# Macaron block (MoE feed-forward, recurrent attention, MoE feed-forward): queries laid out over a dimension of 16, one query load a step, copies, weights and merges issued elsewhere, a new order of the work

## The chip, the core and the metric

One core of a Trainium2 chip runs the whole kernel as one program. The engines are TensorE (PE in the profile, its weight loads PEld), VectorE (DVE), ScalarE (ACT), GpSimd (POOL) and SyncE (SP). SP, ACT and POOL can issue DMAs; the bytes are moved by 16 DMA engines of the core. The metric is the time of one execution on the device in microseconds, the median of several runs.

## The reference, cut to what matters

x is (4, 512, 512) float32. The block is x + 0.5 FFN(LN(x)), then + attention(LN(x)), then + 0.5 FFN(LN(x)).

```python
# FFN: top-2 of E=8 experts with gates, and a shared expert beside them
logits = xf @ gate_w; top2, softmax over the two
h = gelu(xf @ w1[e] + b1[e]);  routed = sum over the two of gate * (h @ w2[e] + b2[e])
shared = gelu(xf @ shared_w1 + shared_b1) @ shared_w2 + shared_b2
# attention: K=32 heads, HH=8 values each, M=8 frequencies, KQ=4 query groups of 8 heads
z = causal_conv4(x @ W_mem);  k_val = z[..., :256], s_raw = z[..., 256:]
q = (x @ W_q).reshape(b, l, 4, 8, 8, 2)                 # group, h, m, re/im
p_w = exp(clip(scale * s_raw, -20, 20) + log_w)          # one weight per head and position
re, im = cumsum(p_w * cos(k_val * theta)), cumsum(p_w * sin(k_val * theta))   # for each m
out_re = sum_m(re * q_re + im * q_im) / den;  out_im = sum_m(im * q_re - re * q_im) / den
y = out_re @ W_re + out_im @ W_im;  (y_val * silu(y_gate)) @ W_out
```

A query group is repeated for its 8 heads: every row of q is used by 8 rows of (head, h).

## The kernel before, in words

**Jobs and groups.** A feed-forward of one batch (512 rows, four tiles of 128) is a job; jobs 0 to 3 are the first feed-forward of batches 0 to 3, jobs 4 to 7 the second. A job fetches its rows into `xin`, normalises them, stores them to DRAM (`x_normal`), turns them, computes the gates and the shared expert (`hidden`, `acc`), and stores the shared part to `sum_rows`. Jobs form groups ([0], [1], [2], [3], [4, 5], [6, 7]) whose rows are sorted by expert into 15 or 23 blocks of 128 rows. For each block POOL gathers rows (`bring`, into three buffers `xs`), TensorE turns them (`x`), multiplies (`one`, L887), turns (`mid`), multiplies (`two`, L903), ACT copies between these, and POOL adds the scaled result to rows in DRAM (`add`, L1698), alternately to `x_rows` and `sum_rows`. The planes `x_rows` begin as copies of x (`w_rows`, L1952), 1 MB for a batch.

**Attention of a batch.** SP loads the rows (`a_load`), POOL adds `sum_rows` to them (`a_add`) and also in DRAM (`m_rows`, L1710, 1 MB read and accumulated). After the norm TensorE makes the memory input (`a_mem`, L922) and the queries (`a_q`, L931), whose weights share one tile `turns_sb` with the output weights, so these are loaded again in turn (`w_head`, L1894 and L1895, and `w_tail`, L1900, on SP). The queries of a group leave TensorE as 128 rows (m, h, re/im); ACT keeps them in `xin`, and SP stores them to DRAM (`q_cols`, L1867) in four DMAs of 256 KB a batch. `xin` is used in turn by jobs and attention (the list `TURNS`), so the next fetch into it waits for these stores.

**Steps.** Then 16 steps (two halves of heads, 8 frequencies) for each batch, 64 in all, one stream on VectorE: phases, ACT's sine and cosine, two scans (L1474), the products with the queries (L1481, L1486), the sums (L1497 to L1507). For each step SP loads `qx` (128 partitions: 2 groups x 8 heads x 8 h; 4 KB each) from `q_cols` in two DMAs of 64 partitions (L1882), each reading 8 different rows 8 times over. After 8 steps the half is scaled by the denominators (`c_out`), moved (L1888) and goes through the gate (`o_gate`, L956) and, after both halves, the output rows (`o_rows`, L965), which POOL adds to `x_rows`. The last job sums them in place.

**Order.** All work is declared as pieces with an engine, a cost, and what they wait for (`plan_job`, `plan_blocks`, `plan_head`, `plan_step`, `plan_tail`); `orders()` lists them for each engine by the length of the way behind them, plus numbers from the table `URGENT`. Each engine executes its list in order; the real waits are on semaphores. Lines that the change and the argument touch most:

```python
# store of a query group, destination in DRAM (SP, L1867)
bass.AP(q_dram, (b % 2 * KQ + q) * P * T, [[T, 2], [2 * T, M * HH], [1, T]])
# load for a step, for g in range(QH) (SP, L1881, L1882)
bass.AP(q_dram, q * P * T + m * HH * 2 * T, [[0, KPQ], [2 * T, HH], [1, 2 * T]])
# normal rows to DRAM (SP, L1845): the same tile xin, [[D, P], [1, D]] as destination
# merge of a batch (POOL): waits for a_loaded[0..3] alone
```

Of the kernel before, what the change touches and what calls it, by code (L numbers as in the profile page):

```python
# [61 lines left out]
def macaron(nc, x, small, gate_w, sw1, sw2, b2_rows, w_experts, w_mem, w_q, w_bd, w_out, out):  # L62
# [43 lines left out]
    with ctx:  # L106
# [146 lines left out]
        q_dram = nc.dram_tensor("q_cols", (2, KQ, M, HH, 2, T), F32)  # L253
# [7 lines left out]
        def batch_rows(dram, b):  # L261
            if isinstance(dram, list):
# [13 lines left out]
                 ("a_load", 2), ("fetch", 4), ("fetch", 5), ("a_load", 3), ("fetch", 6), ("fetch", 7)]  # L276
        work = {}
# [20 lines left out]
        def plan_weights():  # L298
# [8 lines left out]
            piece("SP", ("w_bd",), 0.5, ("PE", ("one", 0, 2)))  # L307
# [3 lines left out]
            for b in range(B):  # L311
                piece("SP", ("w_rows", b), 0.5, ("PE", ("one", 0, 2)) if b >= len(GROUPS[0]) else ("SP", ("w_expert", E - 1)))

        def plan_job(q):
# [10 lines left out]
            piece("POOL", ("load", q), 3.6, ("DVE", ("load", q)))  # L325
# [82 lines left out]
        def plan_head(b):  # L408
            rows, turned_rows = rows_free(("a_load", b))
            if b != 1:  # L410
                piece("SP", ("w_head", b), 0.9, *([("PE", ("o_rows", b - 2, TB - 1))] if b else [("SP", ("w_bd",))]))
            weights = ("SP", ("w_head", 0 if b == 1 else b), 12.0)
# [3 lines left out]
            piece("POOL", ("m_rows", b), 1.0, ("POOL", ("a_add", b, TB - 1)))  # L416
            piece("DVE", ("a_stats", b), 3.4, *[("POOL", ("a_add", b, tb), 4.6 - 0.8 * (TB - 1 - tb)) for tb in range(TB)])
            piece("POOL", ("a_stats", b), 3.6, ("DVE", ("a_stats", b)))
# [31 lines left out]
        def plan_step(i):  # L450
# [3 lines left out]
            piece("SP", ("c_query", b, n), 1.2, *[("SP", ("a_q", b, half * QH + g), 2.5) for g in range(QH)], *free)  # L454
# [8 lines left out]
        def plan_tail(b):  # L463
            if b + 1 < B:
                piece("SP", ("w_tail", b), 0.5, ("PE", ("a_q", b + 1, KQ - 1)), ("PE", ("a_mem", b + 1, 1)))
# [19 lines left out]
            for tb in range(TB):  # L485
                s = ("o_rows", b, tb)
                piece("PE", s, 5.3, ("DVE", ("o_mul", b, VT - 1)), ("SP", ("w_tail", min(b, B - 2)), 15.0),
# [7 lines left out]

        URGENT = {
            ("ACT", "a_q"): {3: 23},
            ("ACT", "a_turn"): {1: 4},
            ("ACT", "acc"): {3: 198},
            ("ACT", "mid"): {1: -298, 3: 19},  # L500
            ("ACT", "o_gate"): {3: -413},
            ("ACT", "one"): {2: 333, 4: -1832},
            ("ACT", "two"): {1: -181, 2: -85},
            ("ACT", "x"): {2: 15, 4: 303},
            ("DVE", "a_stats"): {2: -822},
            ("DVE", "c_sum"): {0: -149, 1: 110, 2: 558, 3: 528},
            ("DVE", "c_times"): {0: -682, 3: 191},
            ("DVE", "c_turn"): {1: -1124, 2: -139},
            ("DVE", "rows"): {2: 217},
            ("PE", "a_mem"): {0: 35, 1: -6, 2: -1076},  # L510
            ("PE", "a_turn"): {1: -815, 2: -510},
            ("PE", "c_out"): {0: -821},
            ("PE", "chunks"): {4: -79, 5: -367},
            ("PE", "gT"): {6: 198},
            ("PE", "hidden"): {2: -6},
            ("PE", "logits"): {6: -852},
            ("PE", "mid"): {0: 271, 1: 960, 3: -444, 4: 344},
            ("PE", "o_rows"): {0: -882, 3: 225},
            ("PE", "one"): {2: 10, 4: -323, 5: -359},
            ("PE", "place"): {1: -674},  # L520
            ("PE", "turn"): {1: 602, 4: 22},
            ("PE", "two"): {1: -8, 3: -104},
            ("PE", "x"): {0: 3, 2: 966, 3: 10, 4: -517, 5: 247},
            ("POOL", "add"): {1: -372},
            ("POOL", "bring"): {1: -163},
        }

# [482 lines left out]
        def scalar_program():  # L1010
# [160 lines left out]

            for stage, *at in ORDERS["ACT"]:
                if stage == "turn":
                    keep_x(*at)
                elif stage == "chunks":
                    keep_chunks(*at)
                elif stage == "gates":
# [879 lines left out]
```

## Time and profile before

| | |
|---|---|
| median of 3 runs | 1193.39 us (1191.97 to 1195.2) |
| the profiled execution, its own time | 1190.12 us |
| its span, first to last instruction | 1188.9 us |
| mean granted TensorE clock | 0.943 |
| TensorE busy | 1024.6 us (86%) |
| VectorE busy | 729.8 us (61%) |
| ScalarE busy | 631.0 us (53%) |
| GpSimd busy | 487.2 us (41%) |

The shares are means over stages that differ: VectorE has no attention steps before 212 us and none behind 954 us, where the last job and the last group are left. Times in the views are us from the start of the span. The granted clock is 1.00 at 2.4 GHz and 0.5 at 1.2 GHz; a mean between them says how much of a stretch was at each level.

### The profile page before, as it was taken

How to read it: one execution, taken by the hardware profiler on the slowest of the kernel's cores; microseconds unless marked ns; L12 is line 12 of the kernel's file. 1: busy time of each engine (PE TensorE's matmuls, PEld its weight loads, DVE VectorE, ACT ScalarE, POOL GpSimd, SP SyncE). 2: the span in 40 equal slices, each digit the busy share in tenths (PEclk: the TensorE clock that was granted, in tenths of full speed). 3: DMA queues.
4: the chain of work that ended last, by engine and by line, in shares of the span. 5: the costliest groups of instructions: out<-in, count | busy, mean ns of one | idle time of the engine just before them, and what ended most of it. 6: DMA issues, size and time to landing. Idle time of an engine off the chain costs nothing.

```text
span 1188.9 us, 11370 instructions
## 1 busy us (share of the span) xinstructions
PE 1024.6 (86%) x3424; PEld 569.3 (48%) x3424; DVE 729.8 (61%) x1210; ACT 631.0 (53%) x1090; POOL 487.2 (41%) x451
## 2 busy tenths in 40 slices
PE   5987989888879979979499989898987899989993
PEld 2465635555344444435255534445453554436661
DVE  2310116878889989879679888998998931200000
ACT  4343325648556588355366574436778852224451
POOL 3434451454553334532432231534363523155642
PEclk9988999998999989989799899898998999999997
DMA  9876571657864666873565757246687645426757
GB/s 311 325 245 158 78 168 49 154 135 159 169 170 105 166 164 109 182 197 107 141 154 117 187 118 178 60 123 180 108 199 164 145 67 77 110 66 130 122 94 113
DMA packets 68977, 172.54 MB, mean 145 GB/s; under 512 B 12354, under 2 KB 12354, under 8 KB 66790
## 3 DMA queue, kind: packets, MB, share of 16 engines
q0 software_dynamic: 32576, 72.44, 33.9%
q1 hardware_dynamic: 36342, 99.38, 27.6%
q8 instruction: 30, 0.49, 0.2%
q14 instruction: 29, 0.24, 0.1%
HBM read 112.86 MB, written 68.33 MB: 152 GB/s over the span
## 4 chain that ended last, share of the span: by engine, by line
PE 29%; DMA 23%; DVE 16%; issue 12%; POOL 11%; ACT 7%; SPq 1%; POOLq 0%; DVEq 0%; ACTq 0%
PE hps L887 8%; PE yps L903 7%; DMA xs<-x_normal,rows_i 4%; DMA x_rows<-ys,rows_i 3%; DMA q_cols<-xin 3%; PE misc L965 3%; DMA xin<-in_x 3%; DVE run L1474 2%; PE xps L878 2%; PE yps L845 2%; DMA qx<-q_cols 2%; PE misc L931 2%; POOL slots L1660 2%; DVE trig L1481 2%; DMA xin<-sum_rows 2%
## 5 line engine op out<-in xcount | busy, mean ns | idle before, releaser
L887 PE MATMUL hps<-w_all,hidden_sb 128*128 x848 | 215.0, 399 | 16.5 <-ACT hidden_sb L1069 13.6
L1674 POOL DMA_INDIRECT xs<-x_normal,rows_i x106 | 128.3, 1210 | 227.8 <-PE xps L878 169.2
L903 PE MATMUL yps<-w_all,hidden_sb 128*128 x424 | 207.8, 614 | 5.7 <-ACT hidden_sb L1069 5.7
L887 PEld LDWEIGHTS hps<-w_all,hidden_sb 128*128 128x128 f32 x848 | 164.5, 201 | 58.1 <-issue 38.4
L1474 DVE TENSOR_TENSOR_SCAN run<-pwx,trig 128x512 f32<-128x512 f32 x128 | 149.5, 1210 | 23.8 <-ACT trig L1157 15.9
L1698 POOL DMA_INDIRECT x_rows<-ys,rows_i x56 | 96.0, 1714 | 118.7 <-ACT ys L1082 112.4
L833 PE MATMUL hps<-xnT,sw_sb 128*128 128x512 f32 x256 | 117.9, 610 | 9.2 <-ACT hidden_sb L1042 9.2
L845 PE MATMUL yps<-sw_sb,hidden_sb 128*128 128x512 f32 x256 | 121.6, 619 | 0.0
L1082 ACT ACTIVATE ys<-yps,slots 128x512 f32<-128x512 f32 x106 | 73.0, 689 | 89.8 <-PE yps L903 72.5
L878 PE MATMUL xps<-ident,xs 128*128 128x128 f32 x424 | 69.7, 292 | 54.5 <-DMA xs<-x_normal,rows_i 25.9
L903 PEld LDWEIGHTS yps<-w_all,hidden_sb 128*128 128x128 f32 x424 | 80.7, 198 | 74.5 <-issue 71.0
L878 PEld LDWEIGHTS xps<-ident,xs 128*128 128x128 f32 x424 | 54.4, 150 | 90.8 <-issue 54.9
L1660 POOL DMA_INDIRECT slots<-told,dest_i x64 | 66.8, 1044 | 57.1 <-DVE cmp_a L1343 38.8
L965 PE MATMUL misc<-turns_sb,tail_sb 128*128 128x512 f32 x192 | 85.3, 593 | 1.8 <-DVE tail_sb L1535 1.7
L1698 POOL DMA_INDIRECT sum_rows<-ys,into_i x28 | 49.6, 1771 | 90.4 <-ACT ys L1082 85.2
L1481 DVE TENSOR_TENSOR trig<-run,qx 128x1024 f32<-128x1024 f32 x64 | 78.0, 1219 | 8.3 <-DMA qx<-q_cols 8.0
L833 PEld LDWEIGHTS hps<-xnT,sw_sb 128*128 128x128 f32 x256 | 48.6, 195 | 70.7 <-issue 59.0
L1060 ACT COPY hidden_sb<-hps 128x256 f32<-128x256 f32 x106 | 39.0, 371 | 78.2 <-PE hps L887 78.0
L1486 DVE TENSOR_TENSOR qx<-run,qx 128x1024 f32<-128x1024 f32 x64 | 78.0, 1218 | 0.0
L845 PEld LDWEIGHTS yps<-sw_sb,hidden_sb 128*128 128x128 f32 x256 | 47.3, 195 | 56.8 <-issue 56.8
L1069 ACT ACTIVATE hidden_sb<-hps,bias_of 128x128 f32<-128x128 f32 x212 | 65.7, 367 | 15.7 <-PE hps L895 15.2
L1052 ACT COPY hidden_sb<-xps 128x512 f32<-128x512 f32 x106 | 62.0, 588 | 19.7 <-PE xps L878 10.9
(202 smaller groups left out, 1530.4 us busy)
## 6 DMA issues: line engine op xcount, KB each, us to landing
qx<-q_cols SPq DMA_DIRECT2D x128, 256.0 KB
w_all<-in_w_experts SPq DMA_DIRECT2D x8, 1024.0 KB, 10.2
x_normal<-xin SPq DMA_DIRECT2D x32, 256.0 KB, 4.2
xin<-x_rows SPq DMA_DIRECT2D x32, 256.0 KB, 7.1
turns_sb<-in_w_out SPq DMA_DIRECT2D x3, 1536.0 KB, 11.5
xin<-in_x SPq DMA_DIRECT2D x16, 256.0 KB, 6.2
sum_rows<-ys SPq DMA_DIRECT2D x16, 256.0 KB, 5.7
xin<-sum_rows POOLq DMA_DIRECT2D x16, 256.0 KB, 8.4
```

The costliest lines, as they stand in the source:

```text
L833: t = PE.matmul(hps[:, bank, :], sw1_sb[:, c, n * P:(n + 1) * P], xnT[:, c, :], start=c == 0, stop=c == KC - 1)
L845: t = PE.matmul(yps[:, bank, :], hT[:, n, tb * P:(tb + 1) * P], sw2_sb[:, n, :], start=False, stop=n == SC - 1)
L878: t = PE.transpose(xps[:, bank, c * P:(c + 1) * P], xs[:, j % NX, c * P:(c + 1) * P], ident[:, :])
L887: t = PE.matmul(hps[:, bank, 0:H], xT[:, j % 2, c, :], w_all[:, bass.ds(expert[j] + c * H, H)], start=c == 0, stop=c == KC - 1)
L903: t = PE.matmul(yps[:, bank, :], hb[:, j % 2, ec, :], w_all[:, bass.ds(expert[j] + (KC * H + ec * D), D)], start=ec == 0, stop=ec == EC - 1)
L965: t = PE.matmul(misc[:, bank, :], yT[:, v, tb * P:(tb + 1) * P], wout_sb[:, v, :], start=v == 0, stop=v == VT - 1)
L1474: t = VE.tensor_tensor_scan(run[:, c, :], pwx[:, n // M, :], trig[:, n % 2, c, :], 0.0, ALU.mult, ALU.add)
L1481: VE.tensor_tensor(trig[:, n % 2, :, :], run[:, :, :], qx[:, n % NQX, :, :], ALU.mult).then_inc(*real_made.of((b, n)))
L1486: VE.tensor_tensor(qx[:, n % NQX, :, :], back, qx[:, n % NQX, :, :], ALU.mult).then_inc(*imag_made.of((b, n)))
L1660: GE.indirect_dma_start(slots_dram[g], bass.IndirectOffsetOnAxis(dest_i[:, g % 2, t, r:r + 1], 0), told[:, g % 2, first_tile + t, r, :], N ...
L1674: GE.indirect_dma_start(xs[:, j % NX, :], None, xn_rows[PAIR_OF[g]], bass.IndirectOffsetOnAxis(rows_i[:, g % 2, j:j + 1], 0)).then_inc(*xs ...
L1698: GE.indirect_dma_start(INTO[g][side], bass.IndirectOffsetOnAxis(at[:, g % 2, j:j + 1], 0), ys[:, j % 2, :], None, compute_op=ALU.add).the ...
```

## The change

1. `q_cols` is laid out as (half, m, group in half, h, re/im, T), so that a store's destination begins with 16 rows (h, re/im) and then 8 (m), and a step's source is 16 rows, each repeated for 8 partitions: one load of 128 partitions and 512 KB instead of two. Partitions of the attention are now ordered (group, h, head) instead of (head, h); the columns of W_mem, taps, theta, norm, W_re and W_im are permuted on the host and the replication matrix `rep_sb` is built with one pass per copy instead of two.
2. The copies of x to `x_rows` for batches 1 to 3 were issued together behind block 2 of group 0; they now stand behind block 8 of group 0, and blocks 2 and 8 of group 1 (the copy to x_normal stays with batch 3's). `bring` waits for that copy only in groups of the second pair of batches. `w_bd` is loaded behind the first attention turn.
3. `w_head` and `w_tail` are issued by ACT instead of SP.
4. `m_rows` on POOL waits for the batch's step 2 besides.
5. `URGENT` is replaced by new numbers, with two further tables (`KINDS` for a kind of piece, `PARTS` for a part of the kernel and its batch), and some costs are changed; so every engine's order is drawn anew.

```diff
-        q_dram = nc.dram_tensor("q_cols", (2, KQ, M, HH, 2, T), F32)
+        q_dram = nc.dram_tensor("q_cols", (2, HALVES, M, QH, HH, 2, T), F32)
+        ROWS_BEHIND = {1: (0, 8), 2: (1, 2), 3: (1, 8)}
...
-            piece("SP", ("w_bd",), 0.5, ("PE", ("one", 0, 2)))
+            piece("SP", ("w_bd",), 0.5, ("PE", ("a_turn", 0, TB - 1)))
...
-                piece("SP", ("w_rows", b), 0.5, ("PE", ("one", 0, 2)) if b >= len(GROUPS[0]) else ("SP", ("w_expert", E - 1)))
+                piece("SP", ("w_rows", b), 0.5, ("PE", ("one", *ROWS_BEHIND[b])) if b in ROWS_BEHIND else ("SP", ("w_expert", E - 1)))
...
-            piece("POOL", ("load", q), 3.6, ("DVE", ("load", q)))
+            piece("POOL", ("load", q), 3.6 if q < 2 else 5.2, ("DVE", ("load", q)))
...
-                piece("SP", ("w_head", b), 0.9, *([("PE", ("o_rows", b - 2, TB - 1))] if b else [("SP", ("w_bd",))]))
-            weights = ("SP", ("w_head", 0 if b == 1 else b), 12.0)
+                piece("ACT", ("w_head", b), 0.4, ("PE", ("o_rows", b - 2, TB - 1) if b else ("one", 0, 2)))
+            weights = ("ACT", ("w_head", 0 if b == 1 else b), 14.0)
...
-            piece("POOL", ("m_rows", b), 1.0, ("POOL", ("a_add", b, TB - 1)))
+            piece("POOL", ("m_rows", b), 1.5, ("POOL", ("a_add", b, TB - 1)), ("DVE", ("c_scan", b, 3)))
...
-            piece("SP", ("c_query", b, n), 1.2, *[("SP", ("a_q", b, half * QH + g), 2.5) for g in range(QH)], *free)
+            piece("SP", ("c_query", b, n), 0.7, *[("SP", ("a_q", b, half * QH + g), 2.5) for g in range(QH)], *free)
...
+        def urgency(k):
+
+            engine, stage, at = k[0], k[1][0], k[1][1] if len(k[1]) > 1 else 0
+            return (URGENT.get((engine, stage), {}).get(at, 0.0) + KINDS.get((engine, stage), 0.0)
+                    + PARTS.get(PART_OF.get(stage), {}).get(at, 0.0))
...
+            def load_head_weights(b):
+                if b > 0:
+                    act.wait_ge(*rows_made.at((b - 2, TB - 1)))
+                else:
+                    act.wait_ge(*one_made.at((0, 2)))
+                SE.dma_start(wmem_sb, w_mem).then_inc(*head_loaded.of((b, 0)))
+                SE.dma_start(wq_sb, w_q).then_inc(*head_loaded.of((b, 1)))
...
-                if g > 0:
+                if PAIR_OF[g]:
                     pool.wait_ge(*rows_filled.at(B - 1))
...
             def merge_rows(b):
+                pool.wait_ge(*scanned.at((b, 2)))
...
-                SP.dma_start(bass.AP(q_dram, (b % 2 * KQ + q) * P * T, [[T, 2], [2 * T, M * HH], [1, T]]),
-                             xin[:, q, :]).then_inc(*q_stored[q].of(b))
+                half, g = divmod(q, QH)
+                into = bass.AP(q_dram, ((b % 2 * HALVES + half) * M * QH + g) * HH * 2 * T,
+                               [[T, 2 * HH], [QH * HH * 2 * T, M], [1, T]])
+                SP.dma_start(into, xin[:, q, :]).then_inc(*q_stored[q].of(b))
...
-                for g in range(QH):
-                    q = b % 2 * KQ + half * QH + g
-                    src = bass.AP(q_dram, q * P * T + m * HH * 2 * T, [[0, KPQ], [2 * T, HH], [1, 2 * T]])
-                    SP.dma_start(qx[g * KPQ * HH:(g + 1) * KPQ * HH, s, :, :], src).then_inc(*q_loaded[s].of((b, n, g)))
+                src = bass.AP(q_dram, ((b % 2 * HALVES + half) * M + m) * QH * HH * 2 * T,
+                              [[2 * T, QH * HH], [0, KPQ], [1, 2 * T]])
+                SP.dma_start(qx[:, s, :, :], src).then_inc(*q_loaded[s].of((b, n)))
...
-                    sp.wait_ge(*one_made.at((0, 2)))
+                    sp.wait_ge(*a_turned.at((0, TB - 1)))
...
-                    if at[0] >= len(GROUPS[0]):
-                        sp.wait_ge(*one_made.at((0, 2)))
+                    if at[0] in ROWS_BEHIND:
+                        sp.wait_ge(*one_made.at(ROWS_BEHIND[at[0]]))
```

## Rows read from the trace of the kernel before

**Rows 1.** Busy times by stretch: PE, PEld, DVE, ACT, POOL, clock, DMA share, GB/s.

```profile
0.00:954.00 954.00, 818.84 (x2689) 449.65 (x2690) 708.62 (x1124) 544.46 (x913) 393.43 (x367) 0.94 0.64 157
218.00:954.00 736.00, 631.06 (x2042) 341.91 (x2041) 652.19 (x955) 458.17 (x753) 305.20 (x242) 0.94 0.63 147
954.00:1188.90 234.90, 205.75 (x738) 119.65 (x736) 21.15 (x87) 86.58 (x178) 93.76 (x84) 0.97 0.53 97
```

**Rows 2.** The chain that ended last, shares of the span by engine.

```profile
PE 29%; DMA 23%; DVE 16%; issue 12%; POOL 11%; ACT 7%; SPq 1%; POOLq 0%; DVEq 0%; ACTq 0%
```

**Rows 3.** The chain in order of time: start us, us, what; nine transfers.

```profile
71.92 10.68 DMA x_rows<-ys,rows_i
83.64 13.99 DMA x_rows<-ys,rows_i
...
160.52 11.15 DMA xs<-x_normal,rows_i
...
201.62 9.30 DMA q_cols<-xin
...
240.00 9.39 DMA q_cols<-xin
249.40 10.12 DMA xin<-in_x
...
340.95 8.87 DMA qx<-q_cols
...
395.60 12.43 DMA xin<-in_x
...
556.07 20.19 DMA q_cols<-xin
```

**Rows 4.** DMA issues: count, KB each, median us from issue to landing.

```profile
x_normal<-xin SPq DMA_DIRECT2D x32, 256.0 KB, 4.2
...
xin<-in_x SPq DMA_DIRECT2D x16, 256.0 KB, 6.2
...
x_rows<-sum_rows POOLq DMA_DIRECT2D x4, 1024.0 KB, 14.6
...
xs<-x_normal,rows_i POOLq DMA_INDIRECT x106, 5.3
...
x_rows<-ys,rows_i POOLq DMA_INDIRECT x56, 5.3
```

**Rows 5.** Waits of VectorE: us in total, times, longest us.

```profile
DVE stats_ffn L1237 <- DMA xin<-in_x: 9.5, 5, 6.4
DVE trig L1481 <- DMA qx<-q_cols: 8.0, 3, 3.5
```

**Rows 6.** SP's issues in order of time, 540 to 560 us.

```profile
543.64 5.21 SPq L1867 DMA_DIRECT2D q_cols<-xin  x2
...
554.23 5.15 SPq L1867 DMA_DIRECT2D q_cols<-xin  x2
```

**Rows 7.** VectorE in order of time, with idle time before and its releaser.

```profile
576.93 2.76 DVE L1237 BATCH_NORM_STATS2 stats_ffn<-xin 128x6 f32<-128x512 f32 x4 [10.60 <-DMA xin<-x_rows]
...
611.88 1.23 DVE L1474 TENSOR_TENSOR_SCAN run<-pwx,trig 128x512 f32<-128x512 f32 x1 [7.21 <-ACT pwx L1148]
```

**Rows 8.** TensorE in order of time, at its longest stall.

```profile
594.26 1.08 PE L878 MATMUL xps<-ident,xs 128*128 128x128 f32 x4 [17.62 <-issue]
```

**Rows 9.** Instructions on qx and on x_rows: ns min/median/max, first and last start.

```profile
L1882 SPq DMA_DIRECT2D qx<-q_cols x128: 567/580/1302, 211.0 to 938.2; - x128
...
L1486 DVE TENSOR_TENSOR qx<-run,qx x64: 1206/1219/1222, 219.4 to 949.1; 128x1024 f32<-128x1024 f32 x64
...
L1710 POOL DMA_DIRECT2D x_rows<-sum_rows x4: 1284/2214/2372, 157.8 to 731.7; - x4
```

**Rows 10.** Waits of SP: us in total, times, longest us.

```profile
SPq L1882 <- DVE outT L1507: 266.6, 40, 16.4
```

**Rows 11.** Busy times in the stretch of the first blocks, columns as in rows 1.

```profile
71.90:98.70 26.80, 17.23 (x67) 11.10 (x65) 0.00 (x0) 7.41 (x19) 9.42 (x8) 0.85 0.95 319
```

More of the change, by code:

```diff
@@ L464, in plan_tail @@
             if b + 1 < B:
-                piece("SP", ("w_tail", b), 0.5, ("PE", ("a_q", b + 1, KQ - 1)), ("PE", ("a_mem", b + 1, 1)))
+                piece("ACT", ("w_tail", b), 0.2, ("PE", ("a_q", b + 1, KQ - 1)), ("PE", ("a_mem", b + 1, 1)))
             rows_before_it = [("PE", ("o_rows", b - 1, TB - 1))] if b else []
@@ L486, in plan_tail @@
                 s = ("o_rows", b, tb)
-                piece("PE", s, 5.3, ("DVE", ("o_mul", b, VT - 1)), ("SP", ("w_tail", min(b, B - 2)), 15.0),
+                piece("PE", s, 5.3, ("DVE", ("o_mul", b, VT - 1)), ("ACT", ("w_tail", min(b, B - 2)), 16.0),
                       bank=[("misc", ("ACT", s))])
@@ L494, in plan_tail @@
                 piece("POOL", s, 1.0, ("ACT", s), ("POOL", ("m_rows", b), 10.0))
-        URGENT = {
[L497 to L525, printed above, removed]
-        }
@@ new lines, in macaron @@
+        PART_OF = {name: part for part, names in (
+            ("job", "fetch load norm turn chunks logits rank gates gT hidden acc"),
+            ("blocks", "place scatter slots rows bring x one mid two add"),
+            ("head", "w_head a_load a_add m_rows a_stats a_norm a_turn a_mem a_p a_fall a_den a_q a_spread"),
+            ("tail", "w_tail c_out o_gate o_mul o_rows o_sum"),
+            ("steps", "c_count c_query c_turn c_scan c_times c_sum")) for name in names.split()}
+        PARTS = {"job": {2: 652, 3: -380, 4: -82, 6: -504},
+                 "blocks": {1: -389, 3: 798},
+                 "head": {},
+                 "tail": {0: -319, 1: 1414, 2: -298, 3: 283},
+                 "steps": {2: 407}}
@@ new lines, in macaron @@
+        KINDS = {("ACT", "mid"): -175,
+                 ("ACT", "norm"): 880,
+                 ("ACT", "o_rows"): 556,
+                 ("ACT", "one"): -59,
+                 ("ACT", "x"): -132,
+                 ("DVE", "a_stats"): -427,
+                 ("DVE", "c_out"): 632,
+                 ("DVE", "c_scan"): -201,
+                 ("PE", "a_mem"): 33,
+                 ("PE", "a_q"): -1,
+                 ("PE", "a_spread"): 1126,
+                 ("PE", "acc"): -144,
+                 ("PE", "gT"): -2768,
+                 ("PE", "hidden"): -415,
+                 ("PE", "logits"): 308,
+                 ("PE", "mid"): 197,
+                 ("PE", "o_gate"): 223,
+                 ("PE", "one"): 7,
+                 ("PE", "x"): 165}
@@ L682, in macaron @@
         y_kept = signal("s_y_kept", BV)
[L684 removed]
+        consts = signal("s_consts", range(14))
         chunk_sums = signal("s_chunk_sums", range(2))
@@ L1174, in scalar_program @@
                     keep_x(*at)
+                elif stage == "w_head":
+                    load_head_weights(*at)
+                elif stage == "w_tail":
+                    load_tail_weights(*at)
                 elif stage == "chunks":
@@ L1942, in sync_program @@
                         SP.dma_start(sum_rows[i][GR:GR + P, :], xs[:, i, :]).then_inc(*cleared.of(NG + 4 + i))
-                elif stage == "w_head":
-                    load_head_weights(*at)
-                elif stage == "w_tail":
-                    load_tail_weights(*at)
                 elif stage == "norm":
@@ L2024, in laid_out @@
                 for vg in range(2):
-                    full[vg, part * 64 + kk * HH:part * 64 + (kk + 1) * HH, kk * NV:(kk + 1) * NV] = \
+                    full[vg, part * 64 + kk:part * 64 + 64:8, kk * NV:(kk + 1) * NV] = \
                         w[8 * g + kk][:, vg * NV:(vg + 1) * NV]
```

76 lines of the change are left out of this document (46 added, 30 removed).

## The prediction

> **What bounds the kernel now.** I first read the busy time by stage. Up to 954 us, where VectorE's last attention step ends, TensorE is busy 818.84 of 954 us; behind it 205.75 of 234.90 us [rows 1]. So TensorE is never far from full, yet 135 us before 954 are idle. In the stretch of the attention steps, 218 to 954, VectorE is busy 652.19 of 736 us and TensorE 631.06. Neither is the bound by itself: VectorE idles 83.8 us there and TensorE 104.9, and the question is what both of them wait for together.
>
> Second, the chain that ended last. Transfers are 23% of it, nearly as much as TensorE's 29% [rows 2]. Its single pieces say which: three stores of queries, q_cols<-xin, at 9.30, 9.39 and 20.19 us (38.9 us together), three loads qx<-q_cols, the longest 8.87 us, and two fetches of x rows begun right behind query stores, 10.12 and 12.43 us. Before all of that stand two additions of expert rows, 10.68 and 13.99 us, and a gather of 11.15 us [rows 3].
>
> Third, what such transfers take elsewhere. A store of the same 256 KB from the same tile xin, x_normal<-xin, lands in 4.2 us (median of 32), a fetch xin<-in_x in 6.2, the gather and the addition of rows in 5.3 each; a merge of a batch takes 14.6 [rows 4]. So the query store is 2.2 to 4.8 times as slow as its twin. The only difference seen in the code is the shape: its destination begins with a dimension of 2, that of x_normal<-xin with one of 128.
>
> Fourth, who pays. VectorE waited 8.0 us for query loads (three times, longest 3.5), 9.5 us for in_x fetches (longest 6.4) [rows 5]. The largest stall is at 556: four query stores are issued in 15.7 us from 543.64 [rows 6], the last takes 20.19 us, the fetch of job 4 waits for it, VectorE stands 10.60 us and then, one attention head later, 7.21 us; TensorE stands 17.62 us [rows 7, 8].
>
> **The change, part by part.** Times are against the profiled execution, 1190.12 us (span 1188.9 and 1.2 around it); the median of the runs, 1193.39, is 3.3 above it, which I add at the end.
>
> Query stores. New destination: dimension 16, then 8; source 128 partitions. I take its price from the twin, 4.2 us, and not 9.3, because bytes, tile and queue are the same and only the outer dimension of 2 goes. (a) At 556: 20.19 - 4.2 = 16.0 us, all of it covered by the idle time of both engines (17.8 on VectorE, 17.62 on TensorE); lower bound 20.19 - 9.30 = 10.9 if only the pile-up of four goes, upper 17.8. I take 16.0. (b) At 240: the store gives 5.2 us and the fetch behind it, once nothing is piled up before it, 10.12 - 6.2 = 3.9, together 9.1; VectorE idled 6.4 in one piece there, so 6.4 (bounds 5.2 and 9.1). (d) At 395: the fetch 12.43 - 6.2 = 6.2; VectorE's other waits for in_x are 9.5 - 6.4 = 3.1, so 3.1 (bounds 0 and 6.2).
>
> The row on that: stores of equal bytes differ 9.30 to 4.2 us by shape alone [rows 3, 4]. The Trainium skill, "DMA: Bandwidth & Descriptors", section "Why a DMA increments its semaphore by 16 and not by 1", says that a DMA is spread over the largest k up to 16 that divides the slowest dimension of both sides, on the lowest-numbered engines: k = 2 for the old store, 8 for the old load, 16 for both new ones. With the page's 27 GiB/s for each engine and about 2 us fixed, an estimate gives 6.6 us for an old store alone, about 20 for four behind one another, and 2.6 for a new one; by it (a) and (b) would each be 1.6 us more, and no other term changes.
>
> Query loads. One load of 128 partitions for two of 64. (c) The three that VectorE waited for come on time if they are 3.5 us sooner at most; one of them also hangs on the store at 201.62. I take all of the wait, 8.0. Lower bound 3.5 (only the one behind the store), upper 3 x (8.87 - 4.2) = 14.0, if each gave back what the longest has in excess. SP issues 64 DMAs fewer, at 0.58 us, so 37 us of SP [rows 9]; it is free: SP waited 266.6 us for VectorE at just this line [rows 10]. What remains is one issue of 0.58 us ahead of each of the three loads on the chain, 0 to 1.7 us, taken as 0 because it lies inside (c).
>
> Together 16.0 + 6.4 + 8.0 + 3.1 = 33.5 us (bounds 19.6 and 47.1).
>
> (e) Copies of x. Before, SP issues three 1 MB copies, one more of x_normal, w_bd and the head's weights at once behind the third block of group 0. The two additions that follow take 10.68 and 13.99 instead of 5.3: 14.1 us in excess. TensorE was busy 17.23 of the 26.80 us there, 9.6 idle, and its granted clock was 0.85 [rows 11], that is some 8 us at the lower of its two levels, 1.2 GHz, of which 5 busy: another 2.6 lost. The clock fell behind the idle time, so it comes back with it. After, only the head's weights are left at this point: 12 us saved (bounds 0 and 14.1). (f) The copies are not gone: three stand behind blocks (0,8), (1,2) and (1,8). The price of one isolated 1 MB transfer beside gathers is seen at 160.52: 11.15 - 5.3 = 5.9 us in excess, behind the merge of batch 0, with TensorE still having shared work in hand, so I count a third, 2 us: 3 x 2 = 6 us lost (bounds 0 and 17.6).
>
> (g) Merges. The same row says what leaving 157.8 saves: 2 us (bounds 0 and 5.9). The other three are moved from one crowded place to another: 0. Each must wait for step 2 of its batch. VectorE's steps lie (949.1 - 219.4) / 63 = 11.6 us apart [rows 9], so batch b's step 2 falls at about 243, 428, 614 and 799 us, against merges at 157.8 to 731.7 now [rows 9]. The work behind it, adding the batch's output rows, comes 13 steps later (150 us, a merge needs 14.6), and the last fetch later still. Head-of-line price: see the rival.
>
> (h) Weights issued from ACT: 9 DMAs; at 0.58 us each 5.2 us of ACT. ACT is busy 458.17 of 736 us, so hidden: 0 (bounds 0 and 5.2). Behind a wait of w_head or w_tail stand ACT's copies and gelus; they wait only if ACT reaches it before TensorE has done the piece named, which the drawn order decides. SP has the time that this gives it to spare (266.6 us, above), so nothing is gained either. Two affine_selects fewer at the start and the permuted columns: 0, nothing waits for rep_sb before the first head.
>
> (i) The order drawn anew. No row prices it. VectorE's idle time in the steps that is not in (a) to (d) is 83.8 - 33.5 = 50.3 us; that is the most that an order could give, and the same amount the most I would give it to lose. I take 0, and a third of it, 17 us, as its spread.
>
> Sum: -33.5 - 12 + 6 - 2 = -41.5; 1190.1 - 41.5 = 1148.6; with 3.3 for the median 1151.9, so **1152 us**.
>
> Does TensorE let it happen? It must do 818.84 us of work before VectorE's last step; in 954 - 41.5 = 912.5 us that is 90% instead of 86%. Yes, but with little to spare. The 234.9 us behind stay as they are: a series of output rows, last job, sorting and 23 blocks.
>
> **The rivals.**
> - Order and layout add up: the new order also fills some of the 50 us. From 22 to 47 us of them, 1105 to 1130; with two thirds, 34 us, 1118. Against it: 818.84 / (912.5 - 34) = 93% TensorE occupation before the last step would be needed.
> - Partial: the time freed goes to TensorE's queue. For it: VectorE and TensorE are both near full between 218 and 954 [rows 1], so a stall taken from one can meet the other's queue. Then of (a) the lower bound, 10.9, and of (e) the 9.6 us of idle time come through: 1193.4 - 20.5 = 1173.
> - The layout does nothing (the slowness of the store is contention: the DMA share at the first blocks is 0.95 [rows 11]). Then (e) - (f) + (g) are left, 8 us, with the order's chance: 1185.
> - Slower: merges hold up POOL. m_rows waits on POOL for a scan, and behind it in the queue stand gathers and additions of blocks. xs has three buffers and a block costs TensorE about 4 us, so 13 us of waiting are covered. The planner counts a step at 8.6 us of VectorE, the trace shows 11.6, so its idea of when the scan comes can be early. To end 4 us above before, the four waits must lose 41.5 + 4 = 45.5, or 11.4 each: POOL held for over 24 us, two steps, each time. Against it: the piece is ordered behind step 3 but waits for step 2 only, one step of slack. At that point: 1197; at three steps each, 34.8 - 13 = 21.8 x 4 = 87 less 41.5: 1239. As a case: 1205.
>
> **How the numbers follow.** Forecast (1130 to 1172): 0.54. Gain with the order: 0.16. Partial (1172 to 1187): 0.13. Layout does nothing, around no change: 0.05. Slower by merges or an order that fits badly: 0.12. A measurement of this kernel tells 0.3%, 3.6 us, from no change. Faster: 0.54 + 0.16 + 0.13 = 0.83; within 0.3%: 0.05; slower 0.12. The range from 1120 to 1188 holds 0.54 + 0.13 + half of the second case and some of the fourth, 0.78.
>
> **What the profile after would show.** q_cols<-xin gone from the chain or near 4 us; no stall like that at 576 to 594 in TensorE; VectorE's waits for qx<-q_cols under 2 us; TensorE's clock near full in the second slice pair; the last step of VectorE near 912 us, with the tail still near 235. Wrong would be: POOL waiting for VectorE's scan at merge_rows for tens of us; the tail grown because TensorE carries unfinished blocks over it; stores still at 9 us.

## The result, and the profile after

The changed kernel takes 1147.06 us (median of 4 runs, 1146.39 to 1149.43) against 1193.32 for the one before: ratio 0.9632, 95% interval 0.9599 to 0.9665, faster by 3.7%. The forecast was 1152 in a range of 1120 to 1188. Its profiled execution has a span of 1145.5 us and a mean granted clock of 0.963 (0.943 before).

Busy times by stretch, columns as in [rows 1], whose three rows the first, second and fourth answer; the third answers [rows 11]:

```profile
0.00:909.00 909.00, 808.56 (x2689) 440.12 (x2690) 706.33 (x1123) 559.17 (x927) 392.61 (x366) 0.96 0.65 165
198.00:909.00 711.00, 633.15 (x2071) 341.94 (x2070) 650.28 (x955) 480.03 (x779) 311.06 (x247) 0.96 0.65 158
70.00:98.70 28.70, 26.31 (x122) 18.78 (x121) 0.00 (x0) 13.32 (x32) 15.74 (x13) 1.00 0.73 176
909.00:1145.50 236.50, 206.22 (x736) 118.89 (x734) 22.13 (x88) 82.88 (x174) 93.60 (x84) 0.97 0.52 96
```

VectorE's last step ends near 909 us, 45 sooner; the tail behind it is 236.5 against 234.9. VectorE's idle time in the steps went from 83.8 to 711 - 650.28 = 60.7 us. TensorE is busy 89% of the time up to the last step. At the first blocks it idles 2.4 us instead of 9.6, at full clock (the stretch begins at 70 us here and at 71.9 in [rows 11]; before, TensorE idled 9.6 us in either).

The waits of VectorE between 198 and 909 us and of SP over the span (us in total, times, longest us), answering to [rows 5, 10]:

```profile
DVE stats_ffn L1283 <- DMA xin<-in_x: 6.6, 4, 2.8
DVE trig L1527 <- DMA qx<-q_cols: 3.9, 1, 3.9
```

```profile
SPq L1926 <- DVE outT L1553: 341.5, 44, 20.5
...
SPq L1880 <- DMA q_cols<-xin: 12.7, 3, 6.4
```

And the instructions on qx, answering to [rows 9]:

```profile
L1926 SPq DMA_DIRECT2D qx<-q_cols x64: 513/527/793, 184.7 to 892.5; - x64
...
L1532 DVE TENSOR_TENSOR qx<-run,qx x64: 1204/1219/1279, 199.4 to 905.0; 128x1024 f32<-128x1024 f32 x64
```

The first step begins 20.0 us sooner (199.4 against 219.4), and the steps lie 11.2 us apart instead of 11.6, which makes 24.1 over the 63 gaps: 44.1 in all. TensorE needs 808.56 us for the work before the tail and needed 818.84 [rows 1], for the same number of instructions: its granted clock there is 0.96 instead of 0.94. Read alone, this looks like a start won by the copies and steps won by the layout. The runs below show that this reading is half wrong: in the old order the copies' start is gone by step 16. The chain of this execution is followed back only to 927 us, so the chains quoted below are those of the experiments.

### The profile page after: what moved, and what is told of

Read it like the earlier page. It is cut to its first block and busy times, and to the rows that moved or that the text cites. A ratio compares the mean times of both kernels' runs of the same rounds, so it can differ in the third digit from the quotient of the medians.

```text
span 1145.5 us, 11321 instructions
## 1 busy us (share of the span) xinstructions
PE 1014.8 (89%) x3424; PEld 559.0 (49%) x3424; DVE 728.5 (64%) x1210; ACT 642.0 (56%) x1100; POOL 486.2 (42%) x449
## 5 line engine op out<-in xcount | busy, mean ns | idle before, releaser
L932 PE MATMUL yps<-w_all,hidden_sb 128*128 x424 | 212.5, 626 | 15.7 <-ACT hidden_sb L1098 15.5
L916 PE MATMUL hps<-w_all,hidden_sb 128*128 x848 | 206.9, 389 | 11.0 <-ACT hidden_sb L1081 10.7
L1720 POOL DMA_INDIRECT xs<-x_normal,rows_i x106 | 121.8, 1149 | 198.9 <-PE xps L907 141.6
L916 PEld LDWEIGHTS hps<-w_all,hidden_sb 128*128 128x128 f32 x848 | 159.7, 195 | 49.4 <-issue 31.1
L1744 POOL DMA_INDIRECT x_rows<-ys,rows_i x56 | 105.2, 1878 | 147.6 <-ACT ys L1111 137.9
L1706 POOL DMA_INDIRECT slots<-told,dest_i x64 | 78.1, 1220 | 51.0 <-DVE cmp_a L1389 32.2
L907 PE MATMUL xps<-ident,xs 128*128 128x128 f32 x424 | 66.8, 283 | 19.0 <-DMA xs<-x_normal,rows_i 6.4
L1183 ACT ACTIVATE trig<-trig 128x512 f32<-128x512 f32 x64 | 40.5, 632 | 54.8 <-DVE trig L1509 53.8
```

The source lines that it names most:

```text
L907: t = PE.transpose(xps[:, bank, c * P:(c + 1) * P], xs[:, j % NX, c * P:(c + 1) * P], ident[:, :])
L916: t = PE.matmul(hps[:, bank, 0:H], xT[:, j % 2, c, :], w_all[:, bass.ds(expert[j] + c * H, H)], start=c == 0, stop=c == KC - 1)
L932: t = PE.matmul(yps[:, bank, :], hb[:, j % 2, ec, :], w_all[:, bass.ds(expert[j] + (KC * H + ec * D), D)], start=ec == 0, stop=ec == EC - 1)
L1706: GE.indirect_dma_start(slots_dram[g], bass.IndirectOffsetOnAxis(dest_i[:, g % 2, t, r:r + 1], 0), told[:, g % 2, first_tile + t, r, :], N ...
L1720: GE.indirect_dma_start(xs[:, j % NX, :], None, xn_rows[PAIR_OF[g]], bass.IndirectOffsetOnAxis(rows_i[:, g % 2, j:j + 1], 0)).then_inc(*xs ...
L1744: GE.indirect_dma_start(INTO[g][side], bass.IndirectOffsetOnAxis(at[:, g % 2, j:j + 1], 0), ys[:, j % 2, :], None, compute_op=ALU.add).the ...
```

## The experiments

The runs that keep the order of before leave every planner cost and table untouched and move single entries of the finished lists, so that no other piece changes its place. Their names begin with b_. Not all runs were taken on the same chip; each ratio is to the kernel before on its own, whose medians there lie between 1192.6 and 1194.3. Where the text below gives the landing of a single transfer that no view lists, it is the time from its issue to the last event of its semaphore in the kept trace, which is how a transfer in the chain gets its length too. One table with all of them; "steps" are the starts of the query products (`trig<-run,qx`) of step 0, of the first steps of batches 1, 2 and 3, and of the last step, in us.

| run | order | median us | ratio to before, 95% | steps |
|---|---|---|---|---|
| before | old | 1193.3 | | 218, 410, 617, 806, 948 |
| b_layout | old | 1150.7 | 0.9647 (0.9583 to 0.9711) | 217, 395, 586, 770, 909 |
| b_store | old | 1171.1 | 0.9804 (0.9738 to 0.9870) | 214, 401, 597, 785, 928 |
| b_two16 | old | 1147.0 | 0.9592 (0.9542 to 0.9642) | 212, 390, 580, 765, 905 |
| b_store8 | old | 1153.9 | 0.9656 (0.9597 to 0.9716) | 212, 396, 586, 770, 911 |
| b_copies | old | 1191.7 | 0.9986 (0.9955 to 1.0017) | 206, 409, 615, 804, 950 |
| b_all | old | 1147.3 | 0.9596 (0.9531 to 0.9662) | 200, 394, 585, 769, 908 |
| b_nomerge | old | 1150.8 | 0.9664 (0.9627 to 0.9700) | 198, 391, 583, 767, 907 |
| b_early | old | 1142.4 | 0.9557 (0.9508 to 0.9606) | 197, 389, 578, 763, 902 |
| the changed kernel | new | 1147.1 | 0.9632 (0.9599 to 0.9665) | 198, 390, 575, 771, 904 |
| order_only | new | 1209.5 | 1.0124 (1.0066 to 1.0182) | 216, 416, 618, 829, 968 |
| new_order_old_shapes | new | 1206.5 | 1.0132 (1.0088 to 1.0176) | 199, 403, 610, 820, 959 |
| new_order_old_copies | new | 1152.2 | 0.9650 (0.9602 to 0.9697) | 212, 398, 582, 777, 909 |
| new_order_early | new | 1144.4 | 0.9594 (0.9560 to 0.9629) | 204, 384, 570, 765, 898 |

**1. The layout alone (b_layout).** q_dram, store, load, waits, `rep_sb` and the host's permutations as in the diff of the change; nothing else.

> The kernel before, with only the layout of the queries: q_cols as (half, m, group, h, re/im, T), stores whose destination begins with 16, one load of 128 partitions a step, the partitions permuted; all five engines keep the order of before. Theory (the layout is most of the gain, terms (a) to (d) of the prediction, 33.5 us): about 1160, between 1149 and 1174; the stall of TensorE at 576 to 594 us gone, no q_cols<-xin over 6 us on the chain. Rival (the order and the moved transfers made the gain, the slow store was contention): 1185 or more, stores still at 9 us or longer.

Measured: 1150.7, 42 us less than the 1192.6 of the kernel before on the same chip, nearly the whole gain of the change, with the lists of all five engines as they were. The theory holds, near the lower end of its range, and the rival (order and moved transfers) falls. No query store or load is among the longest pieces of its chain any more; transfers are 13% of it, 23% before. The stall of TensorE [rows 8] is not gone, as was expected; 6.73 us of it are left, in order of time:

```profile
562.64 1.08 PE L878 MATMUL xps<-ident,xs 128*128 128x128 f32 x4 [6.73 <-issue]
```

**2. Only the stores (b_store).** The layout, but two loads a step:

```diff
-                src = bass.AP(q_dram, ((b % 2 * HALVES + half) * M + m) * QH * HH * 2 * T,
-                              [[2 * T, QH * HH], [0, KPQ], [1, 2 * T]])
-                SP.dma_start(qx[:, s, :, :], src).then_inc(*q_loaded[s].of((b, n)))
+                for g in range(QH):
+                    src = bass.AP(q_dram, (((b % 2 * HALVES + half) * M + m) * QH + g) * HH * 2 * T,
+                                  [[2 * T, HH], [0, KPQ], [1, 2 * T]])
+                    SP.dma_start(qx[g * KPQ * HH:(g + 1) * KPQ * HH, s, :, :], src).then_inc(*q_loaded[s].of((b, n, g)))
```

> As the run with the layout alone, but each step's queries come in two loads of 64 partitions again (8 rows, each repeated 8 times), so only the stores are spread over a dimension of 16. Theory (stores and the fetches behind them are 25.5 of the 33.5 us, loads 8.0): about 1168, 8 us above the run with both. Rival 1 (the loads matter more, since both share the DMA engines with all else): over 1175. Rival 2 (loads are hidden once the store is fast): within 3 us of the run with both.

Measured: 1171.1, between the theory's 1168 and rival 1's 1175: the loads matter more than the theory had it, as rival 1 said, if less than its bound. So the stores are worth 21.6 us and, once the stores are fast, the loads 20.3, not 25.5 and 8. The loads changed with the old stores kept were not run. The chain of this run in order of time (start us, us, what):

```profile
235.96 4.35 DMA q_cols<-xin
240.33 10.23 DMA xin<-in_x
...
262.85 8.56 DMA qx<-q_cols
```

The store has come down from 9.39 to 4.35 us. This piece is one of the slower ones; over all 16 stores the median from issue to landing is 2.9 us (count, KB, us; b_layout has 3.0):

```profile
q_cols<-xin SPq DMA_DIRECT2D x16, 256.0 KB, 2.9
```

The fetch right behind it still takes 10.23, as before (10.12), and a query load 8.56 (the longest before: 8.87). That fetch is the last of the four of job 2, though, and the other three tell more. From issue to landing, in us:

| | fetches of job 2 | first three of job 3 |
|---|---|---|
| before | 14.40, 14.49, 14.89, 10.12 | 11.40, 12.43, 12.21 |
| b_store | 8.03, 8.19, 9.24, 10.23 | 6.88, 6.92, 7.11 |
| b_layout | 6.83, 6.48, 6.63, 6.58 | 4.82, 4.87, 5.05 |

So the slow stores did lengthen most of the fetches behind them, and the slow loads lengthened them further. VectorE's own wait for queries between 198 and 950 us had already shrunk from 8.0 to 2.8 us with the stores alone:

```profile
DVE trig L1481 <- DMA qx<-q_cols: 2.8, 2, 1.9
```

The medians from issue to landing, run b_store first, then b_layout (count, KB, us), say the same of transfers that have nothing to do with queries:

```profile
xin<-x_rows SPq DMA_DIRECT2D x32, 256.0 KB, 6.7
...
xs<-x_normal,rows_i POOLq DMA_INDIRECT x106, 4.8
```

```profile
xin<-x_rows SPq DMA_DIRECT2D x32, 256.0 KB, 5.0
...
xs<-x_normal,rows_i POOLq DMA_INDIRECT x106, 4.4
```

Before, the gather took 5.3 [rows 4]. The query loads are paid by others: fetches, gathers, and TensorE behind them. TensorE gains twice. Up to the tail it idles 103 us instead of 113, and it needs 9.0 us less for about the same work, at a granted clock of 0.96 instead of 0.94 (b_store first, then b_layout; columns as in [rows 1]):

```profile
0.00:933.00 933.00, 819.67 (x2684) 447.17 (x2685) 706.61 (x1123) 544.13 (x912) 392.88 (x365) 0.94 0.66 160
```

```profile
0.00:914.00 914.00, 810.66 (x2694) 443.31 (x2695) 705.22 (x1123) 546.20 (x915) 394.65 (x366) 0.96 0.66 164
```

**3. Is it the shape or the number of loads (b_two16)?** Two loads a step again, but each with all 128 partitions and half of the columns, so that its source begins with 16 rows:

```diff
+                for c in range(2):
+                    src = bass.AP(q_dram, ((b % 2 * HALVES + half) * M + m) * QH * HH * 2 * T + c * T,
+                                  [[2 * T, QH * HH], [0, KPQ], [1, T]])
+                    SP.dma_start(qx[:, s, c, :], src).then_inc(*q_loaded[s].of((b, n, c)))
```

> As the run with the layout alone (1150.7), but a step's queries come in two loads, each of all 128 partitions and one half of the columns, so the source of both begins with 16 rows. It has the issues of the run with only the stores changed (1171.1) and the leading dimension of the run with both. Theory (what costs is the leading dimension of 8, which lengthens other transfers too): within 6 us of 1150.7, gathers and fetches from x_rows as short as there (4.4 and 5.0 us). Rival (what costs is the second DMA of a step, its issue and its packets): about 1171.

Measured: 1147.0, with the 128 issues of b_store and 24 us less than it. The second DMA of a step costs nothing that these runs can tell, so "one load a step" is by itself worth nothing that they can tell. That the leading dimension of 8 is what costs is the theory's reading. The run changes the number of partitions of one DMA with it, from 64 to 128; a load of 64 partitions with a leading 16 was not run, so the two are not told apart by time. The moves of the scaled outputs (`outT<-tail_sb`), also of 64 partitions but with a leading 64, speak for the leading dimension: each ends in 16 semaphore events, as do the transfers with a leading 16 or 128, and a load with a leading 8 in 8 (see the account of the prediction below). The part of the expectation on fetches did not hold: their median was 6.1 us here and 5.0 in b_layout, so single medians of that kind are a weak witness.

**4. A store with a leading 8 (b_store8).** The rows of a query group leave TensorE in another order (host: `transpose(0, 1, 3, 2, 4)`), and

```diff
-                               [[T, 2 * HH], [QH * HH * 2 * T, M], [1, T]])
+                               [[QH * HH * 2 * T, M], [T, 2 * HH], [1, T]])
```

> As the run with the layout alone, but the rows of a query group leave TensorE as (m, h, re/im), so that a store's destination begins with 8 instead of 16. Theory (the time of a store goes down with its leading dimension until other work hides it): within 4 us of 1150.7, since a store under 6 us is hidden; from a leading 2 to 16 the stores were worth 21.6 us, and at 8 four fifths or more of that remain. Rival (only 16 spreads well): 1160 or more.

Measured: 1153.9, 3 us over b_layout, with overlapping intervals. The store on its chain takes 5.44 us, against 4.35 (leading 16) and 9.39 (leading 2). Over all 16 stores the medians are 4.2, 3.0 (b_layout) and 9.6 us (before), and the shortest 4.0, 2.8 and 7.8. The time of the kernel doesn't tell 8 from 16 here.

**5. The copies alone (b_copies).** Waits of `w_rows`, `w_bd` and `bring` as in the change; in SP's list `w_rows` 1 behind `w_head` 0, 2 behind the query of step 4, 3 behind that of step 6, `w_bd` behind the last shared rows of job 1.

> The kernel before, order of all engines kept but for SP, where the copies of x for batches 1 to 3 and w_bd stand where the changed kernel has them. Theory (terms (e) and (f): 12 us saved at the start, 6 lost later): 1187, between 1180 and 1193; TensorE's idle time between 72 and 99 us falls from 9.6 us to under 3, the step stream begins about 10 us sooner. Rival (the 1.6 MB of head weights, still issued there, are enough to lengthen the two additions): start not before 216 us, time within 3 us of before.

Measured: 1191.7: inside the range of the theory, but no gain that can be told from nothing. The start did what was predicted: TensorE is busy 28.59 of 28.70 us between 70 and 98.7 us, the first step begins 12 us sooner (206 against 218). By step 16 it is 1.4 us. The chain shows where it went:

```profile
189.75 9.30 DMA q_cols<-xin
...
231.26 16.80 DMA xin<-in_x
...
262.04 14.28 DMA x_rows<-ys,rows_i
```

SP issues the copy for batch 2 at 230.03 us and the first fetch for job 2 at 230.64, in the same queue. The four fetches take 16.41, 16.80, 16.96 and 12.10 us, each about 2 more than its counterpart before (14.40, 14.49, 14.89, 10.12). The addition of 14.28 begins at 262.04, and the copies for batch 3 are issued at 262.27 and 262.97. The long additions of [rows 3] were moved rather than removed.

**6. Everything but the order (b_all).** Layout, copies, merges behind step 2 (put into POOL's list where the old plan's step 3 ends) and the weights on ACT.

> Every part of the change but the new order: layout, copies, merges behind step 2, weights issued by ACT, with the lists of all engines as before except for the moved pieces themselves. Theory (the order is worth nothing by itself, as in the prediction): 1150 to 1155, within 8 us of the changed kernel's 1147. Rival 1 (the new order gives a third or more of the gain): 1163 or more. Rival 2 (the new order costs, and the mechanics gave more): under 1142.

Measured: 1147.3 against the changed kernel's 1147.1, 3 us under the expected range. With the fast shapes the new order is worth nothing by itself that these runs can tell. A collision at the same place is on its chain:

```profile
221.94 8.80 DMA q_cols<-xin
...
230.76 12.03 DMA xin<-in_x
...
253.40 12.86 DMA sum_rows<-ys,into_i
```

Two transfers of 1 MB meet here, not one: the copy for batch 2, issued at 223.93 us, and the merge of batch 0, which the change has moved to this place by letting it wait for step 2:

```profile
219.72 1.10 POOL L1754 DMA_DIRECT2D x_rows<-sum_rows  x1
```

It starts 17 us before b_layout and is 1.0 us ahead at step 16. Even a store with a leading 16 takes 8.80 us beside them.

**7. The copies earlier still (b_early), then the same in the new order (new_order_early).**

```diff
-        ROWS_BEHIND = {1: (0, 8), 2: (1, 2), 3: (1, 8)}
+        ROWS_BEHIND = {1: (0, 8), 2: (0, 11), 3: (0, 14)}
```

with `w_rows` 2 and 3 directly behind `w_rows` 1 in SP's list.

> As the run with every part but the order (1147.3), but the copies of x for batches 2 and 3 are issued behind blocks 11 and 14 of group 0 (at some 115 and 135 us) instead of near 230 us, where a fetch took 12.03 and an addition 12.86 us. Theory (the lead of 17 us that the copies win at the start was given back because two of them landed on the first steps): 1135 to 1142, the step stream no longer slower than with the layout alone between steps 0 and 16. Rival (the lead is absorbed by something behind it, TensorE's queue or the groups' blocks): within 4 us of 1147.3 with step 16 still at 394 us.

Measured: 1142.4. It reaches step 8 at 284 us, b_all at 294 and b_layout at 298, so half of the theory holds; but only 5 us of that are left at step 16 and at the end. A fetch at 221 us still takes 13.95 us with no copy of x beside it, but the moved merge of batch 0 is still there, and lands in 11.0 us:

```profile
216.09 1.09 POOL L1754 DMA_DIRECT2D x_rows<-sum_rows  x1
```

Intervals of b_early and b_all overlap; the direction is seen in the step table, the size is not settled.

> The changed kernel with the copies for batches 2 and 3 behind blocks 11 and 14 of group 0. In the old order this moved 1147.3 to 1142.4. Theory (the same two transfers disturb the first steps in either order): 1140 to 1144, below both kernels. Rival (the new order was drawn around these places): 1147 or more.

Measured: 1144.4 over 6 runs. The lowest medians of all are these two, but their intervals overlap that of the changed kernel, so neither is shown to beat it.

**8. The new order with the old mechanics (order_only).** Old layout and loads, copies back behind block (0, 2), merges back behind `a_add`; weights stay with ACT.

> The changed kernel's new order with all mechanics of before: queries in the old layout with stores of a leading 2 and two loads of 64 partitions, copies and w_bd behind block (0, 2), merges right behind a_add without the wait; the weights stay with ACT and the partitions permuted. Theory (the order is worth nothing by itself): 1188 to 1198. Rival 1 (the order is a gain that overlaps with the layout's): under 1180. Rival 2 (the order was drawn for the new transfers and is worse with the old ones): over 1200.

Measured: 1209.5, slower than before by 15 us (ratio 1.0066 to 1.0182, small but clear of no change). My theory (worth nothing) falls, and rival 2 holds.

**9. The new order with only the old shapes (new_order_old_shapes).** The store and loads are those of the kernel before, in the new order of partitions:

```diff
-                into = bass.AP(q_dram, ((b % 2 * HALVES + half) * M * QH + g) * HH * 2 * T,
-                               [[T, 2 * HH], [QH * HH * 2 * T, M], [1, T]])
+                into = bass.AP(q_dram, (b % 2 * KQ + q) * P * T, [[T, 2], [2 * T, M * HH], [1, T]])
...
+                    src = bass.AP(q_dram, (b % 2 * KQ + half * QH + g) * P * T + m * HH * 2 * T,
+                                  [[2 * T, HH], [0, KPQ], [1, 2 * T]])
```

> The changed kernel with only the shapes of before: q_cols in the old layout, stores with a leading 2, two loads of 64 partitions a step; the new order, copies, merges and weights stay. In the old order the shapes are worth 42 us. Theory (the new order puts the four stores of a batch closer together, so it loses more when they are slow): 1195 to 1205, that is 48 us or more above the changed kernel, with q_cols<-xin at 16 us or more on the chain. Rival (the excess of the run with the order only came from the copies and merges put back): 1189 or less.

Measured: 1206.5. The shapes that are worth 42 us in the old order are worth 59 in the new one. Its chain holds four stores instead of three:

```profile
199.13 16.79 DMA q_cols<-xin
429.71 23.97 DMA q_cols<-xin
585.09 17.30 DMA q_cols<-xin
...
633.21 17.64 DMA q_cols<-xin
```

The theory's signs came true (48 us or more above the changed kernel, stores of 16 us or more), the time lies 1.5 us above its range. In the old order, two were about 9.3 us, and only those of batch 2 stood close together [rows 3, 6]. Here SP issues the four of the first batch in pairs at 175.94 and 195.47 us with nothing between them but two steps' queries, and the last takes 16.79:

```profile
175.94 7.43 SPq L1911 DMA_DIRECT2D q_cols<-xin  x2
190.75 2.56 SPq L1925 DMA_DIRECT2D qx<-q_cols  x4
195.47 4.17 SPq L1911 DMA_DIRECT2D q_cols<-xin  x2
199.68 16.58 SPq L1880 DMA_DIRECT2D xin<-in_x  x4
```

The store at 585.09 also has another just ahead of it, by 0.6 us. The other two don't: when those at 429.71 and 633.21 are issued, no store of queries is under way, but ACT has issued the 1.5 MB of output weights 0.8 and 1.0 us before. For the first, with a merge issued 3.1 us behind it:

```profile
428.88 0.34 ACTq L1212 DMA_DIRECT2D turns_sb<-in_w_out  x1
429.71 0.55 SPq L1911 DMA_DIRECT2D q_cols<-xin  x1
...
432.85 1.07 POOL L1757 DMA_DIRECT2D x_rows<-sum_rows  x1
```

So the theory's reason, stores closer together, accounts for two of the four. TensorE also pays at the small moves of the scaled outputs (us in total, times, longest us):

```profile
PE misc L985 <- DMA outT<-tail_sb: 33.7, 5, 10.1
```

With the new shapes and the same order, the same wait is 11.0 us in 6. So the new order depends on the fast transfers: it is neither better nor worse with them, and without them 13 us slower than the kernel before, or 15 with copies and merges back in their old places (order_only).

**10. Merges back (b_nomerge) and copies back (new_order_old_copies).**

> As the run with every part but the order (1147.3), but merges right behind a_add, without the wait for step 2. Theory (term (g), 2 us, and no more): within 4 us of 1147.3, a gather of over 9 us back at some 145 us, and POOL waiting nowhere less. Rival 1 (the merges collide four times): 1152 or more. Rival 2 (the wait held up POOL, so taking it away helps): 1143 or less.

Measured: 1150.8, over b_all by 3.5 us with overlapping intervals. The gather beside the merge is back and as long as in [rows 3]:

```profile
144.10 11.29 DMA xs<-x_normal,rows_i
```

and yet the first step begins at 198 us (200 in b_all). The merges' place is worth 3.5 us by the medians, which the overlapping intervals don't tell from nothing. The wait for step 2 did not hold up POOL. What it did is seen at the fetches of job 2, from issue to landing in us:

| run | 1 MB transfer shortly ahead | fetches | step 8 at |
|---|---|---|---|
| b_layout | none | 6.83, 6.48, 6.63, 6.58 | 298 |
| b_nomerge | copy | 8.80, 10.24, 10.80, 11.08 | 287 |
| b_early | merge | 11.53, 13.95, 13.99, 9.04 | 284 |
| b_all | merge and copy | 13.52, 14.65, 15.95, 12.03 | 294 |

Without either, step 8 comes 7 to 10 us sooner than in b_all, 2 to 3 of them won by the first step already. So copy and merge together give back most of the lead by then. Early copies with the merges left in their old place were not run.

> The changed kernel with the copies of x and w_bd back behind block (0, 2), all three at once. In the old order and with the old shapes moving them gave nothing (1191.7 against 1192.6). Theory (what they win at the start is given back before step 16): 1145 to 1151, the first step some 12 us later than 198, step 16 within 4 us of 390. Rival (the new order uses the earlier start): 1155 or more.

Measured: 1152.2, 5 us over the changed kernel, intervals overlapping. The first step is 14 us later, step 16 8 us, the last 5. More of the lead seems to survive in the new order than in the old, as neither theory nor rival had it; the size is not settled.

## Why the prediction was right, point by point

- **The layout is the gain: right, and shown.** Alone it gives 42 us (ratio 0.9583 to 0.9711). Forecast 33.5, bounds 19.6 and 47.1. The forecast took TensorE's 818.84 us before the tail as fixed; 8.2 us of them went too (810.66 in b_layout), as its clock rose from 0.94 to 0.96. No term had that.
- **(a) the stores: right in kind.** With the fetches behind them, (b) and (d), 25.5 us were forecast and 21.6 measured. The price taken from the twin store, 4.2 us, was above the median of 2.9 (4.35 for the one on the chain). Of the 17.62 us stall 6.73 stayed; why, no run shows.
- **(b) and (d), the fetches behind them: right in the main, incomplete.** With fast stores and old loads the fetch of 12.43 us took 6.92, near the 6.2 forecast, and the first three of job 2 fell from 14.4 to 14.9 down to 8.0 to 9.2. But the one fetch that (b) priced, 10.12 us, took 10.23. It took the new loads as well to bring it to 6.58.
- **(c) the loads: mis-sized, and this is the step that failed most.** "The three that VectorE waited for" counted who waits for the transfer and left out whom the transfer delays. Worth 20.3 us once the stores were fast, forecast 8.0, bound 14.0. That the second DMA of a step is free, SP having time to spare, was right (b_two16).
- **The Trainium skill's rule on k** ("DMA: Bandwidth & Descriptors", section "Why a DMA increments its semaphore by 16 and not by 1") puts 2, 8 and 16 engines on the three shapes of store. The traces agree. In the semaphore records, which no view prints, an old store leaves one event about 1 us after its issue and 2 at its end, a store with a leading 8 one and then 8 (in 13 of 16; the other records lack events), and a store with a leading 16 leaves 16. Each old load leaves one and 8, the new load 16. The times fall in that order: medians of 9.6, 4.2 and 3.0 us. The estimate of 2.6 us for a new store is a little low (2.8 to 3.0 in most of b_layout's), and so is that for an old one (6.5 us when worked out again from the same figures, written as 6.6; the shortest took 7.8). No run had four old stores behind one another with nothing else, so the 20 us are not tested; the 20.19 at 556 us began when the first of its four had landed.
- **(e), (f) the copies: the start right, the net wrong.** TensorE's 9.6 us of idle time went and the first step came 12 us sooner in b_copies, as forecast. The loss where the copies land was put at 6 us by a third of one gather's excess; by the end it is as large as the gain: b_copies is 0.9955 to 1.0017 of before. What failed is the price of an isolated 1 MB transfer: it was isolated from the other copies, but not from the fetches issued 0.6 us behind it. The slow shapes hid part of this. Beside them a copy added 2 us to each fetch, and beside the fast ones 2 to 4.5 us (b_nomerge against b_layout).
- **(g) merges: 2 us forecast, 3.5 measured, not told from nothing.** The gather of 11.15 us was saved, as read. What the merge of batch 0 would do where it lands had no price; beside it the fetches of the first steps took 2.5 to 7.5 us more (b_early against b_layout). The rival in which merges hold up POOL is refuted: no wait of POOL for a scan stands among its long ones.
- **(h) weights on ACT: forecast 0.** Not run by themselves. b_all less b_layout, -3.4 us with overlapping intervals, bounds copies, merges and weights together.
- **(i) the order: 0 forecast and 0 measured with the new shapes** (1147.1 against 1147.3). But the model behind it, in which the order has a price of its own beside the layout's, was wrong: with the old shapes the order costs 13 to 15 us. The forecast asked only about one corner of the square.
- **The sum** came out 5 us off, and part of that nearness is luck: errors of both signs met. The layout gave 41.9 us against 33.5 (loads 12.3 more, stores and fetches 3.9 less), and copies, merges and weights together 3.4 against 8. TensorE had room, at 89% up to the last step, and the tail kept its length (236.5), both as predicted.

## What to carry to other kernels

Price a transfer from its twin: same bytes, same tile, another shape. If it is 2 to 5 times as slow, look at the first dimension of both patterns before anything else, and count besides its own waiters all transfers that run beside it. A lead won at the start is only worth what is left of it at the next point where engines meet; read it there (here step 16), not where it was won. And test an order with both versions of what it was drawn for: it can be worth nothing with one and cost 1.3% with the other.

## What the runs showed of the hardware that was not expected

- Query loads with a leading 8 were waited for 8.0 us in all, 2.8 us once the stores were fast, and cost 20 us still. Fetches, gathers and other transfers were longer beside them, and TensorE's granted clock lower.
- The first dimension of a store shows in its semaphore events: 3 for a store with a leading 2, 9 with a leading 8, 16 with a leading 16 (before, b_store8, b_layout). The sixteen stores of 256 KB in each had medians of 9.6, 4.2 and 3.0 us.
- A store with a leading 2 took 7.8 to 11.5 us in 14 of the 16 cases before, and 14.9 and 20.2 us as the third and fourth of four issued in 13 us. In the new order it also took 17.6 and 24.0 us with no other store under way, issued within 1 us behind 1.5 MB of weights.
- Four fetches of 256 KB took 6.5 to 6.8 us in b_layout, 8.8 to 11.1 just behind a 1 MB copy between DRAM tensors (b_nomerge), 9.0 to 14.0 behind a 1 MB merge (b_early) and 12.0 to 16.0 behind both (b_all). Other traffic differs a little between these runs.
- The output weights, 1.5 MB, landed in 11.5 us before and in 11.8 in b_store, both issued by SP (medians of 3); in 9.0 in b_layout, still issued by SP, and in 8.7 in b_all, issued by ACT. So the change in the query loads went with most of the difference, and between the two issuers there is little to see.
